# Causal attention in a macaron block: query tiles and keys from first to last, and the maxima 25 chunks ahead in one stream

## What is computed

```
x = x + 0.5 * ffn(layernorm(x))
x = x + attention(layernorm(x))
x = x + 0.5 * ffn(layernorm(x))

ffn(x):       h = x @ W_exp + b_exp
              h = butterfly(h, up_weights)            # 10 stages of 2x2 mixes
              h = gelu(h + up_bias, exact)
              h = butterfly(h, down_weights)
              y = h @ W_con + b_con + down_bias
attention(x): Q, K, V = x @ WQ, x @ WK, x @ WV        # per head, 16 columns
              scores = Q K^T / 4, causal, softmax over the keys
              y = (probs V) @ WO
```

## Time and profile before

| | |
|---|---|
| median of 3 runs | 2264.9 us |
| the profiled execution, its time | 2265.15 us |
| its span | 2263.4 us |
| PE busy | 2165.8 us, 96% of the span |
| DVE busy | 1652.2 us, 73% |
| ACT busy | 1359.2 us, 60% |
| POOL busy | 251.5 us, 11% |
| mean granted TensorE clock | 0.975 |

### The profile page before, as it was taken

The page is one execution under the profiler, slowest core; times in us unless marked ns, Lnnn a source line. Parts: engine busy times, 40 slices in busy tenths (PEclk is TensorE's granted clock), DMA queues, the critical chain, the costliest instruction groups (busy, mean ns, idle before and its releaser), DMA issues.

```text
span 2263.4 us, 58565 instructions
## 1 busy us (share of the span) xinstructions
PE 2165.8 (96%) x23896; PEld 1224.3 (54%) x23896; DVE 1652.2 (73%) x3827; ACT 1359.2 (60%) x1601; POOL 251.5 (11%) x723
## 2 busy tenths in 40 slices
PE   1799999979999999999999999999999999989999
PEld 1555555434555555555555555555555555556676
DVE  7633344467999999999999999999999994033222
ACT  2432222207787777777877778777777787722321
POOL 7200000000101101111011010110101101100000
PEclk8899999968999999999999999999999999989999
DMA  8012111110111111111111111111111100000000
GB/s 209 1 45 86 52 46 46 46 58 20 44 27 41 37 34 42 31 39 44 27 44 33 35 44 31 39 41 33 41 32 39 44 17 16 2 9 11 19 19 19
DMA packets 68719, 87.28 MB, mean 39 GB/s; under 512 B 20496, under 2 KB 35440, under 8 KB 68208
## 3 DMA queue, kind: packets, MB, share of 16 engines
q1 hardware_dynamic: 67760, 83.45, 14.1%
q0 software_dynamic: 704, 0.25, 0.2%
HBM read 62.15 MB, written 20.97 MB: 37 GB/s over the span
## 4 chain that ended last, share of the span: by engine, by line
PE 92%; DVE 5%; ACT 1%; SPq 1%; issue 0%; DMA 0%; DVEq 0%; ACTq 0%
PE PS L1022 30%; PE PS L1146 29%; PE PS L1004 12%; PE PS L995 8%; PE PS L1126 7%; PE PS L1057 3%; PE PS L1156 1%; PE PS L962 1%; PE PS L1075 1%; DVE OA L747 1%; DVE MXP L803 1%; DVE BNS L699 1%; SPq L353 0%; ACT PG L573 0%; DVE OA L737 0%
## 5 line engine op out<-in xcount | busy, mean ns | idle before, releaser
L632 ACT ACTIVATE PG<-PS 128x1024 f32<-128x1024 f32 (+1 forms) x1152 | 1118.1, 976 | 284.0 <-PE PS L1126 238.4
L803 DVE TENSOR_REDUCE MXP<-PS 128x1 f32<-128x512 f32 x1792 | 1111.9, 685 | 49.6 <-PE PS L1022 46.1
L1022 PE MATMUL PS<-KT,QT 48*128 48x512 f32 (+3 forms) x2304 | 861.1, 440 | 6.6 <-DVE MXP L803 4.9
L1126 PE MATMUL PS<-QT,KT 50*128 50x512 f32 (+1 forms) x2304 | 812.7, 433 | 5.0 <-DMA QT<-MROW 2.9
L1146 PE MATMUL PS<-PG,VH 128*17 128x128 f32 x16896 | 728.0, 276 | 0.4 <-ACT XN L640 0.4
L1146 PEld LDWEIGHTS PS<-PG,VH 128*17 128x17 f32 x16896 | 401.3, 97 | 358.3 <-issue 282.8
L1022 PEld LDWEIGHTS PS<-KT,QT 48*128 48x128 f32 x2304 | 360.3, 186 | 308.9 <-DVE MXP L803 183.1
L1126 PEld LDWEIGHTS PS<-QT,KT 50*128 50x128 f32 x2304 | 341.3, 185 | 20.1 <-issue 19.6
L799 DVE CUSTOM_DVE_ANT_0 PS<-PS,MASK 128x128 f32<-128x128 f32 (+3 forms) x512 | 250.7, 504 | 87.1 <-PE PS L1022 85.9
L518 POOL TENSOR_SCALAR_AFFINE_SELECT PG<-PG 128x128 f32<-128x128 f32 x512 | 137.1, 292 | 1344.1 <-ACT PG L632 1343.3
L1004 PE MATMUL PS<-MD,PG 128*128 128x256 f32 x1024 | 244.8, 388 | 4.2 <-DVE X L770 3.4
(11 more groups left out here) (96 smaller groups left out, 814.1 us busy)
## 6 DMA issues: line engine op xcount, KB each, us to landing
KT<-k_parts SPq DMA_DIRECT2D x256, 64.0 KB
QT<-q_parts SPq DMA_DIRECT2D x256, 64.0 KB
q_parts<-OA SPq DMA_DIRECT2D x16, 512.0 KB, 2.8
k_parts<-OA SPq DMA_DIRECT2D x16, 512.0 KB, 2.7
KT<-k_parts SPq DMA_DIRECT2D x256, 32.0 KB
QT<-q_parts SPq DMA_DIRECT2D x256, 32.0 KB
X<-x SPq DMA_DIRECT2D x8, 512.0 KB, 5.7
out<-X SPq DMA_DIRECT2D x8, 512.0 KB, 2.9
```

Source lines behind the costliest of these rows:

```text
L632: nc.scalar.activation(PB[n % 2][half][:, :, q0:TILE], PS[:, half * 1024:half * 1024 + 1024].rearrange("p (k q) -> p k q", k=2)[:, :, q0:T ...
L803: nc.vector.tensor_reduce(dst, bank(b), AX.X, ALU.max).then_inc(mx_red, 1)
L1022: mm(bank(4 + qs % 2 if b is None else b, w), NQ[0:SC, (BT * j + qs) * P:(BT * j + qs + 1) * P].bitcast(f32r), NK[0:SC, c * TILE:c * TILE ...
L1126: last = mm(PS[:, (2 * half + k) * 512 + q0:(2 * half + k + 1) * 512], CK[0:SM, kb * P:(kb + 1) * P].bitcast(f32r), CQ[0:SM, j * TILE + q0 ...
```

## The change

All orders are turned round and made one stream:

- Query tiles go from 0 to 7, and keys in a tile from key tile 0 to the diagonal, so that the diagonal chunk is a tile's last.
- The maxima run 25 chunks ahead of the scores, over the borders of the heads: the slot of chunk n has the four maxima of chunk n + 25. The first 100 maxima of head 0 lie beside the projections (two more than before), none is alone, and the last 25 chunks of the last head have none.
- The rows of maxima go in two groups of unequal size: tiles 0 to 5 (48 rows: 24 blocks in two parts) and tiles 6 and 7 (16 rows). A group's split is in the slot in which its last maximum is, 25 chunks before the scores of its last chunk: for tiles 0 to 5 in slot 32 of the head before, its transpose in slot 33; for tiles 6 and 7 in slots 11 and 12. For head 0 the first group is done in the last projection stage.
- K and Q are loaded by functions of their own, a slice of K when chunk (7, c) has passed, a tile of Q after its diagonal chunk.
- V of the next head is copied, key tile by key tile, after the values of chunks (7, 0) to (7, 7), the last one after the masks of tile 7.

```diff
-CH = [(j, c) for j in range(NT - 1, -1, -1) for c in range(j, -1, -1)]
+CH = [(j, c) for j in range(NT) for c in range(j + 1)]
...
+AHEAD = 25
+SLOT_N = H * NCH + 2
+M_TILES = ((0, 6), (6, 8))
...
+        def split_slot(i):
+            h, grp = divmod(i, 2)
+            return h * NCH + LAST[M_TILES[grp][1] - 1] - AHEAD + 1
...
+        def rows_in(n):
+            return [i for i in range(1, 2 * H) if split_slot(i) + 1 == n]
...
+            def load_m(i):
+                g = i % 2
+                sp.wait_ge(mt_ev, i + 1)
+                a, b = M_TILES[g]
+                sp.dma_start(CQ[SC:SM, a * TILE:b * TILE].rearrange("p (b t) -> p b t", b=M_BLOCKS[g]), MROW[g][:, :]
+                             ).then_inc(m_ld[g], 16)
...
+            for s in range(-AHEAD, H * NCH):
+                h, n = divmod(s + AHEAD, NCH)
+                j, c = CH[n] if h < H - 1 else (0, 1)
+                if j == NT - 1 or c == j:
+                    sp.wait_ge(mx_ps, h * NMX + BT * (n + 1))
...
+                h, n = divmod(s, NCH)
+                j, c = CH[n] if 0 <= h < H - 1 else (0, 1)
+                if j == NT - 1 or c == j:
+                    sp.wait_ge(st_ps[1], h * NCH + n + 1)
+                    sp.sem_inc(passed[3], 1)
+                    if j == NT - 1:
+                        load_k(CK, h + 1, c, ld_ck[c])
+                    if c == j:
+                        load_q(CQ, h + 1, j, ld_cq[j])
+                for i in rows_in(s - 1):
+                    load_m(i)
...
+            for h in range(H):
+                for j in range(NT - 1):
+                    head_masks(h, j)
+                for c in range(NT):
+                    if c == NT - 1:
+                        head_masks(h, c)
+                    if h < H - 1:
+                        pool.wait_ge(pv_done, h * NCH + CH.index((NT - 1, c)) + 1 + FREE_PB)
                         pool.sem_inc(passed[0], 1)
+                        copy_v(h + 1, c)
...
+            for n in range(H * NCH + 1):
+                if n < H * NCH:
+                    exps(*divmod(n, NCH))
+                for h, j in tile_ended(n - 1):
+                    take_sums(h, j)
...
+                if t == NT:
+                    for k in range(3):
+                        split_step(0, k)
...
-            for seq in range(MX0_ALONE, NMX):
-                n, qs = MX0_ALL[seq]
-                if seq == MX0_START[NT - 1]:
-                    pe.wait_ge(ld_nxt[NT - 1], SLICE)
-                pe.wait_ge(mx_red, seq + 1)
-                maximum(seq, n, qs)
             pe.wait_ge(v_ev, NT * BT + FREE_V)
-            pe.wait_ge(att_init, 2)
             pe.wait_ge(const_rdy, 2)
...
+                for g in range(2):
+                    if half == 0 and c == 0 and j == M_TILES[g][0]:
+                        pe.wait_ge(m_ld[g], h * 16 + 16)
...
+                if c == 0 and half == 0:
+                    pe.wait_ge(os_ev, q)
                 if j == c:
-                    q = h * NT + (NT - 1 - j)
-                    if half == 0:
-                        pe.wait_ge(os_ev, q)
                     pe.wait_ge(masked[half], 2 * q + 2)
...
+            for n in range(SLOT_N):
+                ahead_maximum(n, 0)
+                if n < H * NCH:
+                    scores(*divmod(n, NCH), 0)
+                ahead_maximum(n, 1)
+                if 1 <= n <= H * NCH:
+                    values(*divmod(n - 1, NCH), 0)
+                ahead_maximum(n, 2)
+                if n < H * NCH:
+                    scores(*divmod(n, NCH), 1)
+                ahead_maximum(n, 3)
+                for h, j in tile_ended(n - 2):
+                    turn_sums(h, j)
+                if 1 <= n <= H * NCH:
+                    values(*divmod(n - 1, NCH), 1)
+                for i in rows_in(n):
+                    rows(i)
```

More of the change, by code:

```diff
@@ L306, in program, with tile_ended, splits_in, slot_items @@
         O_SUM = bank(O_BANK, P)
[L308 to L334, removed]
+        def tile_ended(n):
+            h, n = divmod(n, NCH)
+            return [(h, j) for j in range(NT) if 0 <= h < H and LAST[j] == n]
+        def split_slot(i):
+            h, grp = divmod(i, 2)
+            return h * NCH + LAST[M_TILES[grp][1] - 1] - AHEAD + 1
+        def splits_in(n):
+            return [i for i in range(1, 2 * H) if split_slot(i) == n]
+        def rows_in(n):
+            return [i for i in range(1, 2 * H) if split_slot(i) + 1 == n]
+        def slot_items(n):
+            if n + AHEAD < H * NCH:
+                for qs in range(BT):
+                    yield "max", (n + AHEAD) * BT + qs
+            for h, j in tile_ended(n - 2):
+                yield "sums", h * NT + j
+            for i in rows_in(n):
+                yield "rows", i
+        SLOTS = [("rows", 0)] + [i for n in range(SLOT_N) for i in slot_items(n)]
         SLOT_OF = {item: u for u, item in enumerate(SLOTS)}
@@ L526, in _, with copy_v @@
[L526 to L532, removed]
+            def copy_v(h, c):
+                nc.gpsimd.tensor_copy(VH[:, c * BT:(c + 1) * BT, :],
+                                      V[:, c * BT:(c + 1) * BT, h, :]).then_inc(vh_rdy, 1)
@@ L638, in take_sums @@
                 act.wait_ge(pv_done, h * NCH + LAST[j] + 1 + FREE_PB)
-                act.wait_ge(ot_ps, h * NT + (NT - 1 - j))
+                act.wait_ge(ot_ps, h * NT + j)
                 nc.scalar.activation(OS[:, :], O_SUM, ACT.Copy).then_inc(os_ev, 1)
[L642 to L654, removed]
+            for n in range(H * NCH + 1):
[3 more added lines that the diff above has]
+                    take_sums(h, j)
             def o_rows(t):
@@ L1201, in _, with ahead_maximum @@
-            rows(0, 0)
-            scores(0, 0, 0)
-            scores(0, 0, 1)
-            scores(0, 1, 0)
-            scores(0, 1, 1)
-            values(0, 0, 0)
-            values(0, 0, 1)
-            for h in range(H - 1):
-                turn(h, True)
-            turn(H - 1, False)
+            def ahead_maximum(n, qs):
+                if n + AHEAD < H * NCH:
+                    h, k = divmod(n + AHEAD, NCH)
+                    j, c = CH[k]
+                    if qs == 0 and c == 0:
+                        pe.wait_ge(ld_nq[j], h * SLICE + SLICE)
+                    if qs == 0 and c == j:
+                        pe.wait_ge(ld_nk[j], h * SLICE + SLICE)
+                    seq = (n + AHEAD) * BT + qs
+                    slot_free("max", seq)
+                    maximum(seq, k, qs, slot_bank("max", seq))
```

304 lines of the change are left out of this document (110 added, 194 removed).

## The result

The changed kernel takes 2420.7 us in the median (2377.5 to 2442.2, four runs) against 2264.8 for the kernel before (four runs): a ratio of 1.056, 95% interval 1.053 to 1.060. Ratios in this document compare only those runs of a kernel that lie within 1.5% of its fastest, which for the changed kernel are 2377.5 and 2402.3 us. The direction was forecast, the size not: 2273 us stood in the prediction, with 2290 as its upper end. The profiled execution took 2442.21 us.

The account below looks back on a forecast made before the run. The prediction took TensorE (PE), busy for 96% of the span, as the bound, with DVE close behind. Its terms, -41 + 16.8 + 27.8 + 6.8 - 3 + 0.9 = +8.3 on 2265.15, gave 2273 us, range 2259 to 2290.

Parts of the forecast that it names:

- Start, -41: Start of the attention: lone maxima move into the stream, chunk 2 starts at 479.4 instead of 519.24; -41 us (-38 to -44).
- Tile end, +16.8: Tile ends: values wait for ACT's copy until T'+0.82, not 0.66 (T': next chunk's scores start); 112 x 0.15 = +16.8 us.
- Load of the rows, +27.8: Rows of maxima for tiles 0 to 5: late load makes PE wait 1.86 us once per head, 15 x 1.86 = +27.8.
- POOL, +6.8: Head's end: POOL's V copies delay masks; the first delay is covered by the rows' load wait, the second costs 15 x 0.45.
- Small terms, -3: PE's waits for DVE in heads with maxima: pauses give DVE time, the split costs some; -0.2 a head, -3 (-7 to +2).
- Rival B: Clock falls in the new waits: half clock over 6 us costs 2.5, in 6 of 15 heads +15: 2288 us; chance 0.17.
- part 3: The term for the load of the rows of maxima for tiles 0 to 5: PE waits 1.86 us once per head, +27.8.

Follow-up runs that it names:

- both edits: The changed kernel with the load of the rows of maxima issued ahead of the waiting K load, and POOL's masks ahead of its V copies: 2264.6 us.

## Why the prediction was right in its waits and wrong in its time

- **Start, -41: right by luck, then lost.** Chunk 2 starts at 479.49, forecast 479.4, but two errors cancel: chunks 0 and 1 start 1 us earlier than forecast (472.32 and 475.56, forecast 473.3 and 476.6), and chunk 1 takes 3.93 us where I took the middle of 2.45 and 3.2. And the half clock that I had costed at 1 us cost some 13: head 0 took 106.9, and 92.9 in the run without the table load's pause, in which the clock stayed at 1.00. PE's first scores of chunks 0, 1 and 2:

```profile
472.32 0.46 PE L1092 MATMUL PS<-QT,KT 50*128 50x512 f32 x1
...
475.56 0.46 PE L1092 MATMUL PS<-QT,KT 50*128 50x512 f32 x1 [1.12 <-ACT PG L621]
...
479.49 0.79 PE L1092 MATMUL PS<-QT,KT 50*128 50x512 f32 x1
```

- **Tile end, +16.8: right.** The values start at T'+0.80, forecast T'+0.82. With the diagonal chunk first it is T'+0.66 again; 7 x 0.14 of the 1.25 us that a head gains there are this.
- **Load of the rows, +27.8 as a wait: right.** In heads 1 and 2 PE starts 1.9 us late, forecast 1.86; the mean of all fifteen is 2.1 (1.7 to 2.6). From issue to the scores it is 3.67 us (671.20 to 674.87), forecast 3.55. The Trainium skill's page "DMA: Bandwidth & Descriptors" (section "Anatomy of one DMA") gives a fixed cost of about 2.0 us for a DMA issued by GpSimd. This load is issued by SP, so that figure is not its price; the rows of this case are.

```profile
671.20 0.64 SPq L397 DMA_DIRECT2D QT<-MROW  x1
```
```profile
672.93 0.50 PE L985 MATMUL PS<-KT,QT 48*128 48x512 f32 x1
674.87 0.47 PE L1092 MATMUL PS<-QT,KT 50*128 50x512 f32 x1 [1.44 <-DMA QT<-MROW]
```

- **POOL, +6.8: right.** 0.41 us each, forecast 0.45, and the first is indeed covered by the DMA's wait. The second is the row below (scores of that chunk at 677.27, values at 1.06 behind them instead of 0.66); the view names no releaser for it, and that it is POOL is shown by the 0.41 that goes with its masks put first.

```profile
678.33 0.63 PE L1114 MATMUL PS<-PG,VH 128*17 128x128 f32 x14 [0.33 <-issue]
```

- **Small terms, -3: mis-sized.** A head with both edits costs 93.40. Less 91.47 and 1.05 for the tile ends, 0.88 is left, where -0.2 stood: 15 x 1.1 = 16 us where -3 stood. I had named the split that falls on a chunk of four full maxima, and took a gain for it from the pauses. The two slots behind it take 2.86 and 2.80 us, and 2.67 each with the diagonal chunk first, where that chunk is a shorter one.
- **Rival B is the step that failed:** "Half clock over some 6 us costs about 2.5 [...]; in 6 of 15 heads that is +15". Both factors were too small: the clock fell in 13 of 15 heads, and each fall cost 126/12 = 10.5 us in heads 3 to 14. The 6 us are only what was left, behind 519.24, of a low stretch that had begun at 477.6: 47.7 us at half clock, PE busy for 37 of them (first row below). In the changed kernel the stretches last 14 to 68 us, in all runs 10 to 164. I also gave it a chance of its own next to the forecast, as if the forecast's waits could stand without it: in the three profiled runs with a wait of 1.6 to 2.6 us at all fifteen heads it fell at 13, 13 and 11 of them. So part 3's wait stood in the sum at 27.8 us, and the half clock behind it at nothing. The sign was there: the stretch behind the earlier trace rows is at half (second row).

```profile
477.60:525.30 47.70, 37.07 (x126) 16.96 (x126) 28.39 (x61) 7.25 (x8) 1.21 (x5) 0.50 0.13 26
...
1982.80:1989.60 6.80, 6.05 (x14) 4.88 (x15) 1.97 (x5) 0.00 (x0) 0.00 (x0) 0.50 0.00 0
```

Without the clock, an estimate from these runs is -41 + 14 x 4.5 and some 2 for the last head (from its start to the end 377.5 us with the early load, 375.2 in the kernel before): about 2290 us. With the mis-sized small term in it, that is already the range's upper end; the 130 us above it are the clock's. One reading of the rows was off without consequence: six maxima in 3.74 us are 0.62 each and 2.5 a chunk.

## What to carry to other kernels

A stream that keeps PE at full clock must be checked for its longest single pause, not for the sum of its pauses: here a DMA issued 2.8 us too late cost 24 us of waiting and over 100 us of half clock behind it, while the 2.8 us a head that all smaller delays come to (94.3 against 91.5, with the load early) made no fall. Price such a pause by low stretches of the same stream, and where there are none, put the fall into the forecast itself rather than into a rival. Small loads that the next stage waits for go ahead of anything on their queue that itself waits.

## What the runs showed that was not expected

- At half clock a busy PE needs no more idle time to stay there: 36 us at 0.50 in a row with PE busy for 36.00 of 36.00. A busy share near 100% hides it; the granted clock shows it.
- The rate of falls follows the wait: heads late by 1.05 to 1.6 us, 5 of 14; by 1.6 to 2.6 us, 13, 13 and 11 of 15 (the changed kernel, masks first, the late load put back); by over 4 us, all 14. Pauses of 0.15 to 0.45 us, seven or more a head, made none in 14 heads.
- How long a low stretch lasts does not follow the wait: 10 to 27 us behind waits over 4 us, 164 us behind one of 1.66. What ends one isn't shown.
- What a low stretch costs: the window of heads 1 to 14 has a clock of 0.89, so 2 x 0.11 x 1470 = some 320 us at half. The Trainium skill's page "TensorE: Matmul & The Clock Gate" (section "HAM oscillation — how this bites in real kernels") takes half of the throttled time as the penalty, an estimated 160 us; the excess here is 126. A likely reason is that PE does not work at its own pace at full clock either (in a chunk of 2.45 us DVE needs nearly as long for its four maxima), but no run tests it.
- The kernel's time spreads with the falls: 2377 to 2442 us for one binary, where the kernel before, run beside it, stayed within 1.3 us (2256.7 to 2268.2 us in all rounds).
